# A fused two-layer kernel (attention, then routed feed-forward attention): third bf16 parts on VectorE, allocation over two steps, another ramp order

## What is computed

```python
x = x + xattn(layernorm(x), ctx, ctx)      # 16 heads of 16, causal, softmax in f32
x = x + fff_attn(layernorm(x))             # below

def fff(x):                                # one of three trees: q, k and v
    cur = 0
    for _ in range(4):                     # 15 nodes, hard routing
        cur = 2 * cur + 1 + (x . node_w[cur] + node_b[cur] >= 0)
    leaf = cur - 15
    return relu(x @ w1[leaf] + b1[leaf]) @ w2[leaf] + b2[leaf]

q, k, v = fff_q(x), fff_k(x), fff_v(x)
out = softmax(q @ k.T / 16) @ v            # per batch
```

## Time and profile before

| what | us |
|---|---|
| median of three runs | 631.18 |
| the profiled execution, whole | 630.28 |
| its span, first to last instruction | 628.4 |
| TensorE busy | 548.3 |
| VectorE busy | 415.6 |
| GpSimd busy | 351.3 |
| ScalarE busy | 346.0 |
| maxima (L1258), 128 instructions | 121.3 |
| scatters (L1643), 96 instructions | 96.0 |

### The profile page before, as it was taken

One profiled execution on the slowest core, in us unless ns is written; L12 is line 12 of the kernel. 1 busy time (PEld: TensorE's weight loads), 2 busy tenths in 40 slices (PEclk: granted clock), 3 DMA queues, 4 the chain that ended last, 5 costly groups with the idle time before them and its releaser, 6 DMA issues.

```text
span 628.4 us, 15320 instructions
## 1 busy us (share of the span) xinstructions
PE 548.3 (87%) x5389; PEld 451.8 (72%) x5389; DVE 415.6 (66%) x1185; ACT 346.0 (55%) x594; POOL 351.3 (56%) x512
## 2 busy tenths in 40 slices
PE   8667899998989989999977884849999999799996
PEld 7545677876767777777755663748888888688995
DVE  3465777688697797896789763772546565156664
ACT  5226666676566657657644462106888888533331
POOL 6204445456777768767756758513105676666551
PEclk9779999999999999999999886878999999999999
DMA  7998887766996887889755189757999999766663
GB/s 234 252 275 249 261 298 244 243 184 213 282 245 220 270 278 209 265 255 283 217 169 171 68 209 329 197 188 258 364 365 410 392 410 413 274 204 198 194 185 117
DMA packets 107347, 158.55 MB, mean 252 GB/s; under 512 B 12458, under 2 KB 77578, under 8 KB 107274
## 3 DMA queue, kind: packets, MB, share of 16 engines
q1 hardware_dynamic: 95418, 131.02, 65.9%
q0 software_dynamic: 9216, 25.18, 12.2%
q10 hardware_dynamic: 2640, 1.40, 0.7%
HBM read 84.20 MB, written 71.30 MB: 247 GB/s over the span
## 4 chain that ended last, share of the span: by engine, by line
PE 43%; DVE 21%; POOL 10%; issue 9%; DMA 7%; ACT 6%; SPq 4%; DVEq 0%; POOLq 0%; ACTq 0%
DVE mneg L1258 7%; PE banks L869 6%; PE banks L858 6%; PE banks L884 5%; PE banks L930 4%; PE banks L951 4%; POOL xs_dram L1643 4%; PE banks L552 3%; DMA xs_dram<-zero 3%; PE banks L919 2%; POOL rs L1625 2%; PE banks L721 1%; ACT pt L984 1%; PE banks L888 1%; PE banks L602 1%
## 5 line engine op out<-in xcount | busy, mean ns | idle before, releaser
L1258 DVE TENSOR_REDUCE mneg<-banks 128x6 f32<-128x768 f32 x128 | 121.3, 951 | 38.4 <-PE banks L561 37.4
L984 ACT ACTIVATE pt<-banks 128x768 f32<-128x768 f32 x128 | 103.4, 812 | 50.9 <-PE banks L587 47.5
L1655 POOL TENSOR_SCALAR_AFFINE_SELECT pt<-pt 128x512 f32<-128x512 f32 x128 | 81.8, 642 | 84.1 <-ACT pt L984 81.0
L1643 POOL DMA_INDIRECT xs_dram<-xn2s,place x96 | 96.0, 1000 | 52.1 <-PE banks L858 14.3
L559 PE MATMUL banks<-k,q 96*128 96x128 bf16 x256 | 52.0, 226 | 29.2 <-DVE mneg L1258 23.0
L602 PE MATMUL banks<-pt,vp 128*32 128x256 f32 (+1 forms) x1024 | 56.8, 341 | 14.5 <-POOL pt L1655 14.5
L586 PE MATMUL banks<-q,k 98*128 98x256 bf16 x256 | 57.1, 276 | 3.0 <-ACT pt L984 1.1
L559 PEld LDWEIGHTS banks<-k,q 96*128 96x128 bf16 x256 | 25.9, 101 | 42.6 <-DVE mneg L1258 24.2
L602 PEld LDWEIGHTS banks<-pt,vp 128*32 128x32 f32 x1024 | 27.2, 111 | 39.0 <-POOL pt L1655 16.2
L1728 POOL DMA_INDIRECT q_all<-ys_dram,place x32 | 30.8, 963 | 38.5 <-DMA ys_dram<-yb 27.0
L560 PE MATMUL banks<-k,q 124*128 124x128 bf16 x256 | 51.4, 224 | 0.0
(11 more groups left out here) (173 smaller groups left out, 1384.3 us busy)
## 6 DMA issues: line engine op xcount, KB each, us to landing
ys_dram<-yb SPq DMA_DIRECT2D x36, 512.0 KB, 8.3
xb<-xs_dram SPq DMA_DIRECT2D x35, 512.0 KB
xs_dram<-zero SPq DMA_DIRECT2D x45, 256.0 KB, 4.5
xs_dram<-zero SPq DMA_DIRECT2D x18, 384.0 KB, 5.0
parts_dram<-kp SPq DMA_DIRECT2D x16, 384.0 KB, 4.5
k<-parts_dram SPq DMA_DIRECT2D x32, 192.0 KB, 3.5
parts_dram<-qp SPq DMA_DIRECT2D x16, 384.0 KB, 3.6
q<-parts_dram SPq DMA_DIRECT2D x32, 192.0 KB, 3.4
```

What stands on the lines that cost most here:

```text
L984: nc.scalar.activation(pt[:, 2 * p:2 * p + 2, 0:S + P], st_banks(b, p)[:, :, 0:S + P], ACT.Exp, scale=SC / QS).then_inc(exp_sb, 1)
L1258: nc.vector.tensor_reduce(mneg[b % 2][:, 2 * j:2 * j + 2, :], two[:, :, 0:S + P].rearrange("p e (i k) -> p e i k", k=P), axis=AX.X, op=ALU ...
L1643: gp.indirect_dma_start(xs_dram[tree], bass.IndirectOffsetOnAxis(ap=place[:, k:k + 1], axis=0), xn2s[m % RING][:, t, :], None).then_inc(sc ...
L1655: pool.affine_select(out=diag, in_=diag, compare_op=ALU.is_ge, fill=0.0, base=0, pattern=[[0, 2 * T], [1, P]], channel_multiplier=-1).then ...
```

## The change

- `third_part` is issued by VectorE (q at j=4, after the maxima of the place and ahead of `divide(b, 0)`; k at j=6, after the maxima), no longer by GpSimd.
- For pairs, allocation part 6 moves from j=6 of the even step to j=1 of the odd step after it, and part 7 from j=1 to j=6 of that odd step (in step 13 both stand at j=1, since group 5 begins there). Single batches keep part 6 at j=6.
- The first batch of a pair is scattered at places 2 to 7 of its step, since its addresses come later.
- Zero pages 14 are issued a step earlier (step 13); 15 and 16 in step 14, 17 and 18 in step 15.
- In the ramp the constant rows of buffer 1 are two ScalarE copies of 32 x 4096 instead of two DMAs; q of batch 0 is unloaded ahead of k of batch 1; `load_x(3)`, `load_c(3)` and the constant rows of buffer 2 are issued later; `norm_in(3)` stands after the fourth maxima and `norm_out(3)` ahead of the q parts of batch 2.

The diff:

```diff
@@ -58,6 +58,7 @@
 GROUPS = [(m, m + 1) for m in range(0, 10, 2)] + [(m,) for m in range(10, NB)]
 MAXT = 2 * T
 SLOTS = 0, 1, 2, 4, 5, 6
+FIRST_SLOTS = 2, 3, 4, 5, 6, 7
 NAL = 25
 NPLACE = 20
 PIECES = 4
@@ -392,14 +393,14 @@
                     load_x(b + 4)
                 if b == 0:
                     sp.wait_ge(consts, NCONST)
-                if b <= NB:
+                if b < NB - 2:
                     zero_pages(b)
+                for ahead in {NB - 3: (NB - 2,), NB - 2: (NB - 1, NB), NB - 1: (NB + 1, NB + 2)}.get(b, ()):
+                    zero_after(ahead)
                 if b in (1, 2):
                     zero_pages(b - 3)
                 if b == 0:
                     load_b2()
-                if b == NB + 1:
-                    zero_after(b + 1)
                 if has(b, -1):
                     load_xr(b - 1, 1 - u)
                 if has(b, -2):
@@ -427,8 +428,6 @@
                         sp.wait_ge(st_ps, PAIRS * (NB - 1))
                         for k in range(2):
                             load_table(1 if b <= NB else 2, (b - NB + 1) % 2 * 2 + k)
-                    if b == NB:
-                        zero_after(b + 1)
 
             def const_fill(z, full, wide):
 
@@ -449,26 +448,23 @@
                 const_fill(0, q4, qw4)
                 sp.wait_ge(unloaded[0], 16)
                 stack(0, 0, ms=(1,))
+                unload(0, 0)
                 unload(1, 1)
-
-                unload(0, 0)
+                stack(0, 1, ms=(1,))
+                unload(1, 0)
+                sp.wait_ge(unloaded[0], UNLOADS)
+                for c in range(C):
+                    stack(0, c, ms=(0,))
                 load_x(3)
-                stack(0, 1, ms=(1,))
-                sp.wait_ge(unloaded[0], UNLOADS)
-                stack(0, 0, ms=(0,))
-                unload(1, 0)
-                stack(0, 1, ms=(0,))
-                const_fill(1, k4, kw4)
-                const_fill(1, q4, qw4)
-                load_c(3)
                 sp.wait_ge(unloaded[1], UNLOADS)
                 for c in range(C):
                     stack(1, c)
+                load_c(3)
                 load_x(4)
+                unload(2, 1)
+                unload(2, 0)
                 const_fill(2, k4, kw4)
                 const_fill(2, q4, qw4)
-                unload(2, 1)
-                unload(2, 0)
 
             ramp()
             pipeline(step)
@@ -565,7 +561,7 @@
                 if j % 4 == 0:
                     pe.wait_ge(stacked[j // 4][b % BUFS], landed(b, j // 4))
                 if j == 0 and b < BUFS:
-                    pe.wait_ge(const_rows[b], 32)
+                    pe.wait_ge(const_rows[b], 2 if b == 1 else 32)
 
             def scores(b, n, u, j):
 
@@ -1116,12 +1112,16 @@
                 nc.scalar.copy(vp[0][:].rearrange("p t h c -> p (t h) c")[:, :, 0:DK],
                                G7[:].rearrange("p (m c) -> p m c", c=DK)).then_inc(v_sb, 1)
                 norm_out(2)
+                act.wait_ge(q_factor, WIDE + 1)
+                for full, narrow in ((k4, kw), (q4, qw)):
+                    nc.scalar.copy(full[1][KS:P, :, :].rearrange("p h (i k) -> p (h i) k", k=P),
+                                   narrow[KS:P, :].unsqueeze(1).to_broadcast([P - KS, NH * T, P])).then_inc(const_rows[1], 1)
                 first_part(kp, K1, W_BANKS[0], k_ps, 2, k1_sb, 1.0)
                 copy_xnT(2)
+                norm_out(3)
                 first_part(qp, Q1, G7, q_ps, 2, q1_sb, QS)
                 second_part(kp, K2, k_rem, kr_sb, 2, k2_sb)
                 second_part(qp, Q2, q_rem, qr_sb, 2, q2_sb)
-                norm_out(3)
 
             ramp()
             pipeline(step)
@@ -1227,6 +1227,11 @@
                 ge(v, third_sem, b)
                 nc.vector.scalar_tensor_tensor(rem[:], ps[:], scale, part[b % 2][:, slot, :], ALU.mult, ALU.subtract
                                                ).then_inc(rem_sem, 1)
+
+            def third_part(b, part, slot, second, rem, ready, done):
+
+                v.wait_ge(ready, b + 1)
+                nc.vector.tensor_tensor(part[b % 2][:, slot, :], rem[:], part[b % 2][:, second, :], ALU.subtract).then_inc(done, 1)
 
             def residual(b, n, u):
 
@@ -1298,18 +1303,27 @@
                         divide(b, 1)
                     if j == 3 and b < NB and group_after(b) is not None:
                         allocate(group_after(b), 3)
+                    if j == 4 and has(b, LEAD):
+                        third_part(b + LEAD, qp, Q3, Q2, q_rem, q2_sb, q3_sb)
+                    if j == 6 and has(b, LEAD):
+                        third_part(b + LEAD, kp, K3, K2, k_rem, k2_sb, k3_sb)
                     if j == 3 and has(b, LEAD + 1):
                         norm_in(b + LEAD + 1, n + 2, u)
                     if j == 3 and has(b, LEAD):
                         remainder(b + LEAD, G7, kp, K1, k_rem, k1_sb, k3_sb, kr_sb, 1.0)
                     if j == 3 and b < NB and group_after(b) is not None:
                         allocate(group_after(b), 4)
-                    if j in (5, 6) and b < NB and group_after(b) is not None:
-                        allocate(group_after(b), j)
+                    if b < NB and group_after(b) is not None:
+                        if j == 5:
+                            allocate(group_after(b), 5)
+                        if j == 6 and len(GROUPS[group_after(b)]) == 1:
+                            allocate(group_after(b), 6)
+                    if b < NB and j == 1 and group_after(b - 1) is not None and len(GROUPS[group_after(b - 1)]) == 2:
+                        allocate(group_after(b - 1), 6)
                     if j == 2 and b > NB:
                         for part in (5, 6, 7):
                             allocate(group_after(b), part)
-                    if j == 1 and b < NB and group_after(b - 1) is not None:
+                    if b < NB and group_after(b - 1) is not None and j == (6 if group_after(b) is None else 1):
                         allocate(group_after(b - 1), 7)
                     if j == 6 and b == NB - 1:
                         allocate(group_after(b), 7)
@@ -1428,11 +1442,6 @@
                     v.wait_ge(alloc, al(g, 24))
                     tt(owner[:], owner[:], inside1[:], ALU.add).then_inc(alloc, 1)
 
-            def third_part(b, part, slot, second, rem, ready, done):
-
-                v.wait_ge(ready, b + 1)
-                nc.vector.tensor_tensor(part[b % 2][:, slot, :], rem[:], part[b % 2][:, second, :], ALU.subtract).then_inc(done, 1)
-
             def k_parts(b, ps):
                 remainder(b, ps, kp, K1, k_rem, k1_sb, k3_sb, kr_sb, 1.0)
                 third_part(b, kp, K3, K2, k_rem, k2_sb, k3_sb)
@@ -1457,9 +1466,10 @@
                 q_parts(0, G7)
                 q_parts(1, W_BANKS[0])
                 norm_in(2, 1, 0)
-                norm_in(3, 1, 1)
                 for j in range(PAIRS):
                     first_maxima(j)
+                    if j == 3:
+                        norm_in(3, 1, 1)
                 last_maxima(0)
                 remainder(2, W_BANKS[0], kp, K1, k_rem, k1_sb, k3_sb, kr_sb, 1.0)
                 remainder(2, G7, qp, Q1, q_rem, q1_sb, q3_sb, qr_sb, QS)
@@ -1628,7 +1638,11 @@
 
             def scattered_in(b):
 
-                return [m for m in (b - 5, b - 4) if 0 <= m and (b - m == 5) == (len(GROUPS[group_of(m)]) == 2)]
+                return [m for m in (b - 5, b - 4) if 0 <= m and b - m == (5 if len(GROUPS[group_of(m)]) == 2 else 4)]
+
+            def slots_of(m):
+
+                return FIRST_SLOTS if len(GROUPS[group_of(m)]) == 2 and m == GROUPS[group_of(m)][0] else SLOTS
 
             def scatter(m, tree, ts=range(T)):
 
@@ -1643,11 +1657,6 @@
                     gp.indirect_dma_start(xs_dram[tree], bass.IndirectOffsetOnAxis(ap=place[:, k:k + 1], axis=0),
                                           xn2s[m % RING][:, t, :], None).then_inc(scat[tree][m % RING], 16)
 
-            def third_part(b, part, slot, second, rem, ready, done):
-
-                gp.wait_ge(ready, b + 1)
-                pool.tensor_tensor(part[b % 2][:, slot, :], rem[:], part[b % 2][:, second, :], ALU.subtract).then_inc(done, 1)
-
             def causal(b, p):
 
                 gp.wait_ge(exp_sb, PAIRS * b + p + 1)
@@ -1659,23 +1668,20 @@
                 for j in range(PAIRS):
                     if j == 0 and has(b, -1) and b < NB:
                         causal(b - 1, 4)
-                    if j == 5 and has(b, LEAD):
-                        third_part(b + LEAD, kp, K3, K2, k_rem, k2_sb, k3_sb)
                     if has(b, 0) and j >= lag(b):
                         causal(b, j - lag(b))
                     if j < LAG and has(b, -1):
                         causal(b - 1, j + PAIRS - LAG)
-                    if j in SLOTS and b < NB - 1:
+                    if b < NB - 1:
                         for m in scattered_in(b):
```

(7 more changed lines are left out.)

## The result

| | kernel before | changed kernel |
|---|---|---|
| median, us | 631.02 (4 runs) | 637.22 (4 runs, 636.33 to 637.93) |
| profiled execution, whole | 630.28 | 636.33 |
| its span | 628.4 | 634.2 |

The account below looks back on a forecast made before the run. Odd steps were taken as bound by TensorE's work, allocating even steps by its waits for VectorE's maxima. -3.7 - 1.4 + 5.6 + 2.4 - 2.3 = +0.6 us on 630.28 gave 630.9; forecast median 631.8 us, range 628.0 to 635.2.

Parts of the forecast that it names:

- Third parts, 0: Pipeline steps: VectorE's added third parts, 0.69 us each, stay covered without TensorE waiting in either kind of step; 0 us.
- Part 6 out of the even steps, -3.7 and -1.4: Steps 4, 6, 8, 10: the 0.92 us wait before the next scores goes, -3.7 us; step 12's likewise, -1.4 us.
- Part 6 into the odd steps, +5.6: Maxima of j=2 come 2.1 us later; steps 7, 9, 11 lose 1.5 us each, step 5 1.1; +5.6 us.
- about 0.5 us of ScalarE's lag is room that the shift can use up: Odd steps, between k projection and k_rem: about 0.5 us of the 2.1 us shift is absorbed.
- nothing absorbed: Slower rival's odd steps: no shift absorbed behind the k projection, 2.1 us lost each, 8.0 us instead of 5.6; chance 0.32.
- Step 13, +2.4: Step 13: parts 6 and 7 together at j=1, VectorE hiding little; +2.4 us, bounds 1.1 and 3.1.
- Ramp, -2.3: Ramp: norm of batch 3 ahead saves 1.8 us, earlier first scores 0.5, ScalarE's copies stay hidden; -2.3 us.
- The 0.5 for earlier first scores: Ramp: q of batch 0 unloaded ahead of k of batch 1 starts the first scores earlier; 0.5 us gained.
- the clock does not fall: Faster rival's ramp: step 0's q projection runs at 2.4 GHz, 1.8 us more gained; rival at 628.3 us, chance 0.28.
- Zero pages, 0: Steps 13 to 15: issuing zero pages earlier neither gains nor costs; 0 us, bounds -1 and +1.
- slower rival: Part 6 at j=1 decides: odd steps lose 8.0 us, step 13 3.1; sum +3.7 or +3.2; 634.4 us, chance 0.32.
- the ramp gives nothing: Addition to the slower rival: if the ramp's ScalarE copies are slower than estimated, its gain vanishes; 636 us.

Follow-up runs that it names:

- e1: Kernel before with only the allocation's move (part 6 of a pair to j=1 of the odd step, first batch's scatters to places 2 to 7): ratio 1.0096.
- e2: Kernel before with only the third parts moved to VectorE: ratio 1.0036.
- e12: e7 with GpSimd's reciprocal roots ahead of mask and scatter, and the routing tree's three products behind a step's last maxima: ratio 0.9781 to the kernel before.
- e14: e12 with the third parts of q and k back on GpSimd: ratio 0.9805 to the kernel before.
- e7: Changed kernel, pair's part 6 split: four instructions at even j=6, five at odd j=1, last pair's whole in step 12: ratio 0.9961 to the kernel before.
- e8: Changed kernel with only the last pair's part 6 back in step 12: ratio 1.0035 to the kernel before.
- e3: Kernel before with only the ramp's edits (ScalarE copies, SyncE's new order, norm of batch 3 ahead): ratio 0.9966.
- e16: Kernel before with TensorE kept busy by multiplications of ones (96 and 68) in the ramp's two idle times: ratio 0.9945.
- e10: Changed kernel with TensorE kept busy by multiplications of ones (96 and 36) in the ramp's two idle times: ratio 1.0001 to the kernel before.
- e6: Kernel before with part 4 of the allocation behind the maxima of j=4 instead of ahead of them: ratio 1.0032.
- e9: Kernel before with only the zero pages' new order: ratio 1.0008.
- e15: Kernel before, allocation unmoved, with GpSimd's roots first and the routing tree's three products behind a step's last maxima: ratio 0.988.
- e11: Changed kernel with ScalarE's two copies of the constant rows ahead of the norm of batch 2: ratio 1.0073 to the kernel before.
- e5: Changed kernel with GpSimd's reciprocal roots of the next norm ahead of the mask and scatter of j=4: ratio 1.0085 to the kernel before.

## Why the prediction was wrong, point by point

- **Third parts, 0: near the measured sum in the changed kernel, by luck.** Two terms put at nothing cancel: the shortened hold gives 0.33 us in each of steps 6, 8 and 10, and the longer mask takes 0.15 in an odd step (e1 against the change). "In neither does TensorE come to wait" holds only with part 6 gone from j=6: alone they cost 0.36% (e2). In an even step of e12 the shortened hold outweighs them by 0.5 us (e14).
- **Part 6 out of the even steps, -3.7 and -1.4: measured -5.4 and -1.5.** The wait of 0.92 went, as said. Another 0.46 us for each of steps 6, 8 and 10 went with it, which no wait row had shown: 0.31 is the earlier start of the scores of j=7, which belongs to the third parts, and 0.15 lies between the transposes of the normalized batch and the next scores, which is open. The reading that VectorE is the busiest engine in steps 12 and 13 is right for step 13 only; in step 12 TensorE is busy for 19.57 us and VectorE for 18.14.
- **Part 6 into the odd steps, +5.6: the step that failed, measured +8.9.** The shift of 2.1 us was right, and so was the wait before the scores of j=3 (1.5 to 2.1 said, 2.15 measured). What failed is "about 0.5 us of ScalarE's lag is room that the shift can use up". That room is on the branch k_rem, maxima of j=4, scores of j=5, and there it is gone: k_rem starts 1.61 us later in its step, with the projection 2.14 later, and no wait is left at j=5. (In e7 ScalarE's lag is gone too, with no late projection, so it was not simply room; there the roots of j=1 start 1.2 us earlier in their step than in the kernel before, with the scatters of j=0 and 1 gone ahead of them.) But the same late projection delays, through TensorE's order, the exponential, the mask, the scatter, the roots, the norm and the next exponential, and that branch has no room: TensorE waited 0.23 us at its end in the kernel before, and waits 0.90 in the change. It made the loss 2.31 in steps 7, 9 and 11, the whole shift and 0.17 for the longer mask. The forecast had set GpSimd aside by its busy time (16.1 to 16.2 us), but this chain runs through it. The rival "nothing absorbed" had the size, 2.1 for each, but kept to the chain through k_rem.
- **Step 13, +2.4: measured +3.7,** above its own upper bound of 3.1. Nothing was hidden in VectorE's idle time, which grew from 2.0 to 2.9 us in the step; TensorE waited 2.92 us for the maxima of one pair. Its clock fell too (0.93 in the window of the step). e8 takes 4.3 us back. What the part above 3.1 is made of is open.
- **Ramp, -2.3: in the profiled execution 0, in runs of it alone -2.2 us (e3), with the clock held -0.6 to -0.9 (e16, e10).** The start of step 0 moved by 1.76 us, which is near the 1.8 read from VectorE by luck: 2.71 us were gained behind the first scores and 0.95 lost ahead of them. The 0.5 for earlier first scores is wrong: they start at 25.8 to 26.8 us in nine traces with the new order and no filling, at 25.3 to 26.1 in six with the old one (before, e1, e2, e6, e9, e15). The copies took 3.60 us each and not 3.4; ahead of the norm they gained nothing (e11). And "the clock does not fall" was thought of as an extra gain only; that a low stretch can last longer and take a gain back was not in the range.
- **Zero pages, 0: right** (e9).
- **Range.** The three misses of the sum (+3.3, +1.3, +2.3) outweigh the one of the other sign (-1.8), and all lie on the side of the slower rival, whose price of 634.4 kept the ramp's gain. With its own "the ramp gives nothing" it was 636, and by its own terms (+3.7, and the 2.3 of the ramp taken off again) 637.2; either lies outside the stated range, though the range was said to take in both rivals.

What the change was to cure, the wait at an even step's end, did not need part 6 to move: three small products stood ahead of the maxima that TensorE waits for, and nobody waited for them (e15, e12; no run moved them alone).

## What to carry to other kernels

When a late piece is said to be absorbed, follow every chain that starts at it, not the one that was late before: a shift is absorbed only if each branch has room. Before moving a long piece into another step, look at what stands ahead of the awaited result and is itself awaited by nobody; moving that costs nothing. A ramp's gain is read over several executions with the granted clock beside it, and filling TensorE's idle time there was worth more here (0.5% to 0.9%) than reordering it (0.3%).

## What the runs showed of the hardware that was not expected

- The granted clock fell to 1.2 GHz inside a running pipeline, behind waits of only 2.0 to 2.2 us, in each odd step from 5 to 11 of e5, in steps 5 and 7 of e1 and e11, and in none of steps 4 to 12 of the profiled change. The projection behind the wait then takes 2.72 to 3.59 us instead of 1.97.
- ScalarE copied 32 partitions by 4096 bf16 columns in 3.60 us, 0.88 ns a column.
- A VectorE instruction on 48 columns was stretched from 0.20 to 1.28 us beside a GpSimd instruction that began 0.03 us behind its start (e14).
- The other way round, a mask of GpSimd took 0.83 us instead of 0.64 beside a VectorE instruction with two inputs in SBUF that began 0.35 us before it (step 9 of the change against e1).
